# A Hyena layer in a vision tower: three band buffers, moved sums, gated products summed by four column groups and reordered through DRAM

## What is computed

```python
u = jnp.einsum('bld,ed->ble', inputs, w_in) + b_in
...  # short filter of three taps; split by head into x0, x1, v
kv = x1[..., i] * v[..., j]          # outer product of the channels of a head
y[i] = x0[j] * causal_conv(kv[i, j], h)   # summed over the j channels of the head
...  # RMS norm over the 192 channels, then w_out, b_out and the residual
```

## Time and profile before

| | us |
|---|---|
| median of 3 executions | 706.13 |
| lowest, highest | 704.66, 707.17 |
| the profiled execution | 707.24 |
| its span, first to last instruction | 705.5 |
| mean granted clock of PE in it | 0.975 of full speed |
| PE, DVE, ACT, POOL busy | 598.2, 286.9, 199.4, 146.3 |
| the Hyena part, from PE's first turn of rows to the first rows for the router | 498.8 to 593.8 |

### The profile page before, as it was taken

The page is one execution under the profiler, slowest core; times in us unless marked ns, Lnnn a source line. Parts: engine busy times, 40 slices in busy tenths (PEclk is TensorE's granted clock), DMA queues, the critical chain, the costliest instruction groups (busy, mean ns, idle before and its releaser), DMA issues. The chain is left out here.

```text
span 705.5 us, 10938 instructions
## 1 busy us (share of the span) xinstructions
PE 598.2 (85%) x4299; PEld 434.5 (62%) x4305; DVE 286.9 (41%) x662; ACT 199.4 (28%) x479; POOL 146.3 (21%) x215
## 2 busy tenths in 40 slices
PE   1023979999999989878999999999867999979996
PEld 1001749555555543334999999989534557649995
DVE  0000042467768647796043333345395125202221
ACT  2001242144444433242434443310341002112220
POOL 6771110011111102342000000002063212312222
PEclk9999999999999999999999999999997999989998
DMA  7506132000000000410987777100633791346650
GB/s 200 170 5 266 71 102 68 1 1 1 2 1 1 2 0 1 133 47 1 320 315 296 291 293 276 68 1 1 243 130 88 279 342 67 108 158 194 187 174 1
DMA packets 26667, 86.55 MB, mean 123 GB/s; under 512 B 7182, under 2 KB 16551, under 8 KB 21498
## 3 DMA queue, kind: packets, MB, share of 16 engines
q1 hardware_dynamic: 23946, 82.70, 33.8%
q0 software_dynamic: 2672, 3.17, 1.6%
HBM read 79.49 MB, written 7.04 MB: 123 GB/s over the span
## 5 line engine op out<-in xcount | busy, mean ns | idle before, releaser
L1556 DVE TENSOR_TENSOR eo<-banks,soft_factors 32x192 f32<-32x192 f32 x128 | 45.3, 354 | 91.7 <-PE banks L1506 71.0
L1537 ACT ACTIVATE ex<-banks,soft_b 128x128 f32<-128x128 f32 x192 | 51.2, 399 | 73.3 <-PE banks L1492 73.2
L889 DVE TENSOR_REDUCE nm<-banks 128x1 f32<-128x453 f32 x96 | 55.9, 624 | 31.6 <-PE banks L662 31.3
L1506 PE MATMUL banks<-soft_pair_w,ex 128*128 128x192 f32 x384 | 66.4, 330 | 1.4 <-issue 1.4
L680 PE MATMUL banks<-qa,kt 32*99 32x256 f32 (+1 forms) x384 | 65.9, 399 | 0.0
L849 ACT ACTIVATE pt<-banks 128x1024 f32<-128x1024 f32 (+1 forms) x48 | 49.1, 1023 | 57.2 <-PE banks L680 57.2
L662 PE MATMUL banks<-kt,qt 32*128 32x453 f32 x192 | 62.5, 590 | 2.3 <-DVE nm L889 0.9
L1506 PEld LDWEIGHTS banks<-soft_pair_w,ex 128*128 128x128 f32 x384 | 62.0, 190 | 3.3 <-issue 1.6
L1487 PE MATMUL banks<-slots_a,soft_pair_w 128*128 128x128 f32 x384 | 45.9, 276 | 1.2 <-PEq L1256 1.1
L1487 PEld LDWEIGHTS banks<-slots_a,soft_pair_w 128*128 128x128 f32 x384 | 44.9, 192 | 2.4 <-issue 2.0
L680 PEld LDWEIGHTS banks<-qa,kt 32*99 32x99 f32 (+1 forms) x384 | 38.3, 172 | 4.0 <-issue 0.8
(11 more groups left out here) (297 smaller groups left out, 1003.6 us busy)
## 6 DMA issues: line engine op xcount, KB each, us to landing
soft_pair_w<-in_spair SPq DMA_DIRECT2D x32, 1152.0 KB, 7.4
hy_band<-in_hband SPq DMA_DIRECT2D x6, 1540.0 KB, 6.7
route_tile_wi<-in_wi SPq DMA_DIRECT2D x15, 576.0 KB
switch_wo<-in_wo SPq DMA_DIRECT2D x1, 4608.0 KB, 15.6
hy_x_spread<-x_rows SPq DMA_DIRECT2D x24, 128.5 KB, 5.2
sorted_x<-blank_rows SPq DMA_DIRECT2D x15, 193.0 KB
route_tile_x<-sorted_x SPq DMA_DIRECT2D x15, 193.0 KB
vt<-in_vt SPq DMA_DIRECT2D x1, 2496.0 KB
```

The lines of the kernel that those rows point to most:

```text
L889: dve.tensor_reduce(nm[:, n % 2, j, at:at + 1], ps[:, q, 0:NK], AXX, ALU.max, negate=True).then_inc(maxed, 1)
L1506: mm = pe.matmul(ps[:, 6 + q, 0:D], hid[:, p % 2, q, j, :], w[:, at:at + D], start=j == 0, stop=j == HJ - 1)
L1537: ins = act.activation(hid[:, p % 2, q, j, :], hidden(p, q, j), ACT.Gelu, bias=k.b1[:, 2 * p + q, j:j + 1])
L1556: dve.tensor_tensor(eo[SL * r:SL * (r + 1), b, i, :], ps[SL * b:SL * (b + 1), 6 + e % 2, 0:D], b2[SL * r:SL * (r + 1), i, :], ALU.add).the ...
```

## The change

Eight things are changed, all in the Hyena layer:

- POOL's two sums to `h` go from behind outer(1) to behind outer(3); outer(1) now waits for the second third's kvz.
- DVE runs `cls_outer(0)` and `cls_outer(1)` ahead of the next tap step each, and PE's `pick_cls(0)` goes ahead of a product.
- There are three band buffers and three x0 buffers instead of two (the third x0 buffer and both `hy_kv` buffers lie in the switch layer's `route_tile_wi`, which is idle then); SP interleaves band and x0 loads and loads the output weights behind them.
- There are six buffers of gated products instead of three.
- `sum_y` is replaced for groups 0 to 4 by `sum_pairs`: when all four pairs of a group are gated, four matmuls with a 32-column selection matrix write to four column groups, 32 rows each, of one bank. Its rows stand in another order (pair, then image). Group 5 keeps the old form (`sum_last`).
- ACT copies such a bank to `hy_y_by_pair`, stores its four quarters to a DRAM tensor `y_rows` and, once all four are stored, loads them back in the old order into `hy_y`.
- The squares of groups 0 to 4 are first added up by POOL (`add_squares`, behind all outer products; slots of two and a sum), and PE handles them once; the last group's are handled as before. ACT waits for POOL's add before it overwrites a slot.
- PE's `project(0, c)`, and DVE's class rows of y, wait for the load of that group (`y_moved`).

```diff
 for g in range(NG):
     if g % 2 == 0:
         pool.wait_ge(x.xr, 4 * (g // 2 + 1))
+    if g == 1:
+        pool.wait_ge(x.kvz_r, 2)
     if g >= 2:
         pool.wait_ge(conv, GP_ * (g - 1))
     for s in range(JT):
         outer(g, s)
-    if g == 1:
+    if g == 3:
         pool.wait_ge(x.wout_in, 32)
         pool.tensor_tensor(k.h[:, :, :], k.h[:, :, :], bc(x.bout[:, :], 1, NT),
                            ALU.add).then_inc(h0, 1)
         pool.wait_ge(h0, 1)
         pool.tensor_tensor(k.h[:, :, :], k.h[:, :, :], k.xn[:, :, :], ALU.add).then_inc(h1, 1)
+for c in range(1, NG - 1):
+    add_squares(c)
...
+def add_squares(c):
+    pool.wait_ge(ysq_r, c + 1)
+    if c >= 2:
+        pool.wait_ge(ysa_r, c - 1)
+    pool.tensor_tensor(ysq[:, 2, :], ysq[:, 0 if c == 1 else 2, :], ysq[:, c % 2, :], ALU.add
+                       ).then_inc(ysa_r, 1)
...
+def sum_pairs(c):
+    wait_y_bank(c)
+    pe.wait_ge(gated, GP_ * (c + 1))
+    for g in range(GP_):
+        mm = pe.matmul(ps[QUAD * g:QUAD * (g + 1), YB + c % 2, 0:L], x.sel_pair,
+                       prod[:, (GP_ * c + g) % PR, :], start=True, stop=True)
+    mm.then_inc(ysum, GP_)
...
     cls_source(m)
     cls_source(m + 1)
     convolve(m)
-    if m >= 2:
-        sum_y(m - 2)
-        sum_y(m - 1)
     convolve(m + 1)
+    if m % GP_ == 0 and m >= GP_:
+        sum_pairs(m // GP_ - 1)
+    if m == PAIRS - 2:
+        sum_last(PAIRS - 4)
+        sum_last(PAIRS - 3)
...
-    if m >= GP_ and m % GP_ == 2:
-        squares(m // GP_ - 1)
-sum_y(PAIRS - 2)
-sum_y(PAIRS - 1)
+pe.wait_ge(ysa_r, NG - 2)
+squares(2, x.image_pair, x.tail_pair, True)
+sum_last(PAIRS - 2)
+sum_last(PAIRS - 1)
...
 for c in range(NG - 1):
-    pe.wait_ge(y_r, c + 1)
+    pe.wait_ge(y_moved[c % 2], 16 * (c // 2 + 1))
     project(0, c)
...
+def store_y(c):
+    r = c % 2
+    act.wait_ge(yp_r, c + 1)
+    if c >= 2:
+        act.wait_ge(y_moved[r], 16 * (c // 2))
+    for g in range(GP_):
+        act.dma_start(y_rows[r, :, g, :, :], y_pair[QUAD * g:QUAD * (g + 1), r, :]
+                      ).then_inc(y_stored[r], 16)
+def load_y(c):
+    r = c % 2
+    act.wait_ge(y_stored[r], 16 * GP_ * (c // 2 + 1))
+    act.dma_start(y[:, c, :], y_rows[r].rearrange("b g n l -> (b g n) l")).then_inc(y_moved[r], 16)
 for c in range(NG):
     act.wait_ge(ysum, GP_ * (c + 1))
-    act.activation(ysq[:, c, :], ps[:, YB + c % 2, 0:L], ACT.Square).then_inc(ysq_r, 1)
+    if c >= 2:
+        act.wait_ge(ysa_r, max(1, c - 2))
+    act.activation(ysq[:, c % 2, :], ps[:, YB + c % 2, 0:L], ACT.Square).then_inc(ysq_r, 1)
...
+    act.activation(y_pair[:, c % 2, :], ps[:, YB + c % 2, 0:L], ACT.Copy, scale=x.nw_pair[:, c:c + 1]
+                   ).then_inc(yp_r, 1)
+    store_y(c)
+    load_y(c)
```

More of the change, by code:

```diff
@@ L1639, in __init__ @@
         self.x1, self.v = (sb(n, [P, JT, NH * B * CH]) for n in ("x1", "v"))
[L1640 to L1641 removed]
+        self.band = sb("band", [P, BRING, HG, BANDW])
+        spread = sb("x0_spread", [P, 2, GP_, L])
+        self.xrep = [spread[:, 0, :, :], spread[:, 1, :, :],
+                     k.route.wi[2][:, 0:GP_ * L].rearrange("p (u l) -> p u l", u=GP_)]
         consts = sb("consts", [P, MIXC])
@@ L1709, in sync @@
         sp.dma_start(x.consts[:, :], a["hconsts"]).then_inc(x.const_in, 16)
[L1710 to L1713, removed]
+        x.load_band(sp, a, 0)
         sp.wait_ge(x.c2, W_X0 + 1)
@@ L1716, in sync @@
         sp.wait_ge(x.x0_out, 16)
-        for g in range(2):
-            x.load_x0(sp, g)
+        x.load_x0(sp, 0)
+        x.load_band(sp, a, 1)
+        x.load_x0(sp, 1)
+        sp.dma_start(x.wout[:, :, :], a["hwout"]).then_inc(x.wout_in, 16)
+        sp.dma_start(x.bout[:, :], a["hbout"].broadcast_to([P, D])).then_inc(x.wout_in, 16)
+        x.load_band(sp, a, 2)
+        x.load_x0(sp, 2)
         sp.wait_ge(x.c2, W_X0_REST + 1)
@@ L1879, in stage_hyena @@
         rms = sb("hy_rms", [P, NT])
-        zeroed, kv_r, conv, gated = (k.sem(f"hy_{n}") for n in ("zeroed", "kv_ready", "conv", "gated"))
+        zeroed, kv_r, conv, gated, ysa_r, yp_r = (k.sem(f"hy_{n}") for n in (
+            "zeroed", "kv_ready", "conv", "gated", "squares_added", "y_by_pair"))
+        y_stored = [k.sem(f"hy_y_stored{r}") for r in range(2)]
+        y_moved = [k.sem(f"hy_y_moved{r}") for r in range(2)]
+        y_rows = nc.dram_tensor("y_rows", (2, B, GP_, 2 * CH, L), F32, kind="Internal").ap()
         ysum, y_r, ysq_r, yc_r, ms_m, mse_r, rms_r = (
@@ L1890, in _ @@
                 k.route.load(sp, a)
-                for g in range(2, NG):
-                    sp.wait_ge(conv, GP_ * (g - 1))
+                for g in range(BRING, NG):
+                    sp.wait_ge(conv, GP_ * (g - BRING + 1))
                     x.load_band(sp, a, g)
-                    sp.wait_ge(gated, GP_ * (g - 1))
+                    sp.wait_ge(gated, GP_ * (g - BRING + 1))
                     if g == P // (2 * CH * GP_):
@@ L1978, in squares, with sum_last @@
+                def sum_last(m):
+                    if m % GP_ == 0:
+                        wait_y_bank(NG - 1)
+                    pe.wait_ge(gated, m + 1)
+                    pe.matmul(ps[:, YB + (NG - 1) % 2, 0:L], x.sel[:, m % GP_, :], prod[:, m % PR, :],
+                              start=m % GP_ == 0, stop=m % GP_ == GP_ - 1).then_inc(ysum, 1)
+                def squares(slot, image, tail, first):
+                    if first:
                         pe.wait_ge(zeroed, 1)
```

109 lines of the change are left out of this document (63 added, 46 removed).

## The result

The changed kernel takes 703.23 us (median; 700.01 to 706.75) against 707.62 for the kernel before on the same chip (704.49 to 709.87), a ratio of 0.9943, 95% interval 0.9921 to 0.9964. Faster, as forecast, but by 4.4 us instead of the 9.1 that the sum gave, and just above the range of 689 to 703 (the measured median is 703.2; 0.9943 of 706.13 would be 702.1).

The account below looks back on a forecast made before the run. Bound: DVE's chain with POOL's sums before the Hyena loop, then PE alone to 586.6. With ACT's round trip as the new limit, shift -10.6 plus 1.5 clock loss gave -9.1: 698.1, or 697.0 as median; range 689 to 703.

Parts of the forecast that it names:

- A, the start: Before the Hyena loop: PE's first class row at 523.5, 9.6 us earlier, without the gap, convolutions then at 2.4 GHz.
- B, PE's loop: PE's Hyena loop: the sum over four column groups takes 0.64 us, so a group takes 5.98 us instead of 8.22.
- step D: ACT's DRAM round trip: 5.65 us a hop, 4.8 more for group 2's stores beside the weights; last load lands at 575.6.
- C: POOL's add behind its last outer product makes ACT wait: group 2's square starts at 552.0, not at 546.3.
- the rival of held products: POOL's moved sums hold DVE's gated products 3.8 us twice, PE stalls 2 to 3 us: 699.5 us; chance 0.05.
- E: Fifth projection step: load of y at 575.6 against 586.24, shift -10.6; clock loss 1.5, so -9.1 us in sum.
- Quiet stores: ACT's stores slip between the weight rows: no 4.8 us delay, clock loss 0.5, so -14.9, 691.2 us; chance 0.25.
- Long hops: Stores of one group queue behind each other, 5.2 us instead of 2.5 in three hops: -4.8, 701.3 us; chance 0.13.
- Slower than before: Every DRAM hop costs 11.0 us, group 4's load lands at 590.1: +6.4 with the clock, 712.5 us; chance 0.03.

Follow-up runs that it names:

- The repeat: The changed kernel run once more, unedited, on the chip of the experiments; ratio to the kernel before 0.9954.
- start-only kernel: The kernel before with only the moved POOL sums and outer(1), and the earlier DVE and PE class steps; ratio 0.9873.
- the first two with ACT freed: The changed kernel with each group's load behind the next group's stores and separate square slots; ratio 0.9801 with expert weights late, 0.9886 with them early.

## Why the prediction was right and wrong

**A, the start: right.** 523.5 predicted for the first class row, 522.93 measured, full clock, no gap. (The repeat has no gap either, but its clock fell behind the first gated product.) The first gated product cost PE 1.31 us, not 0.6. In the start-only kernel A came to 7.1 us of stage, where that product's wait was 1.94 and half clock followed, so some of the 9.6 was given back there.

**B, PE's loop: right.** 0.64 for the sum over four column groups. PE's rows of the sum stand at 533.65, 539.26 and 544.87, 5.6 apart, a little under 5.98. The gain couldn't be cashed, as step D below says.

**C: right in size, wrong in place.** POOL's rows:

```profile
539.02 3.85 POOL L1952 TENSOR_TENSOR h<-h,hy_b_out 128x1728 f32<-128x1728 f32 x1
542.95 3.85 POOL L1955 TENSOR_TENSOR h<-h,xn 128x1728 f32<-128x1728 f32 x1
546.76 4.29 POOL L1923 TENSOR_TENSOR route_tile_wi<-hy_x,hy_v 128x512 f32<-128x512 f32 x4
551.01 0.63 POOL L1938 TENSOR_TENSOR hy_y_square<-hy_y_square 128x257 f32<-128x257 f32 x1
```

The add ends at 551.6, where I had 551.75. The cover of outer(4) was thin by 0.41 us (PE's wait for it at 549.07) instead of spare by 0.6. But ACT didn't come for the third square until 566.91; it was held by the stores and not by this add. Without the late bands it happened as foretold: third square 17.3 us after the first (547.00 - 529.70), predicted 552.0 - 534.3 = 17.7. Gated products beside the sums kept their 0.42, so the rival of held products is out:

```profile
541.60 0.43 DVE L2152 TENSOR_TENSOR hy_prod<-banks,route_tile_wi 128x257 f32<-128x257 f32 x1 [1.80 <-PE banks L1985]
```

**D failed, in one term: which stores are congested, and by how much.** I gave groups 0 and 1 quiet stores and charged group 2 with 4.8. I had asked only what the weight load would do, dated it right (546.5, measured 545.47), and then put the wrong store beside it and cut the hold off at 562.1, its landing when it took 15.6 us as before. Three terms were wrong:

- The bands, which I had put at nothing. A quicker PE brings 1.5 MB every 5.6 us, and group 0's stores met them: 9.15 us instead of 2.16.
- Group 1's stores, at 548, were the ones beside the weights, and were held to their end: 16.28 us.
- That end is 566.3, for the weights are slowed too, and land in 20.8 us instead of 15.6.

The high bound should have been: a store issued behind the weights may be through only when they are, and nothing in the trace of before spoke against that. With group 1 held to 566.46, group 2 began at 566.91 instead of 552.0, 14.9 later, and the 4.8 charged to it fell away. From its square to the last load's issue it was 15.4 us (566.91 to 582.31) and not 16.4, and that load took 2.0 and not 2.4: 14.9 - 4.8 - 1.0 - 0.4 = 8.7. It was through at 584.3, and predicted for 575.6. Of the excess of 21.1, the add at 552.0 would have covered 6.4 in any case (552.0 - 534.3 - 2 x 5.65).

**E: right in size, wrong in what PE waits for.** PE was to wait some 4 us before the squares and, longest, before the fifth projection step, for the load of y. Before the squares it did wait, 3.04 us; for the load of y it never did. The end of the chain in the trace of the change, from POOL's last add on:

```profile
577.94 0.65 POOL hy_y_square L1938
578.63 0.39 PE banks L2017 x2
...
582.18 3.51 PE banks L2057 x40
```

PE waits for POOL's last add, and then works at half clock (0.50 from 580 to 584): the five projection steps take 3.51 us, where they took 1.84, and it comes to the fifth at about 582.18 + 4/5 of 3.51 = 585.0, when the load has been there for 0.7 us. Both the add and the load hang on the same square of group 4 (577.47), so the late stores are to blame either way. At full clock the load would have set the end, 584.3 + 1/5 of 1.84 = 584.7; PE ended at 585.7. So the clock cost 1.0, for which I took 1.5. The end of the steps is 0.9 earlier than before (586.61), and so are the router's rows (592.27 and 593.13), where the sum had 9.1.

**What lies behind the stage** I had left as it was, and it gave 3.6 us in the first pair of traces and 1.6 in the second (112.4 to 110.8). Of the 3.6, 1.3 is the landing of the last scatter (POOL's idle time before the first tile 6.16, then 4.89, with the scatters issued alike) and most of the rest PE's clock: in the windows from 626 to 632, before and after,

```profile
626.00:632.00 6.00, 4.91 (x26) 4.24 (x28) 0.00 (x0) 1.40 (x6) 0.19 (x1) 0.50 0.37 111
```

```profile
626.00:632.00 6.00, 5.22 (x53) 4.70 (x52) 1.11 (x2) 1.77 (x7) 0.00 (x0) 1.00 0.35 120
```

PE did 26 matmuls at half speed, or 53 at full. Why the unedited part fares better is open. The kernel before with late weights had 111.1 there, so it isn't bound to the change. Of the difference between the spans, then, the stage has a quarter in the first pair of traces (1.1 of 4.5) and half in the second (2.2 of 4.3). That the measured time came so near the range is luck: 9.1 was forecast for the stage, and 1.1 and 2.2 (88.66 to 86.43) came.

**The rivals.** Quiet stores would have been 14.9 us faster, and with weights late and no late bands the stage was 16.3 shorter: the mechanism was computed about rightly, its condition wasn't met. "Long hops" came nearest in time, 701.3, by another mechanism: hops weren't all long, two were very long. The chance on it was too small because I had taken the congestion as a matter of one hop. "Slower than before" has a slip in its sum: with hops of 11.0 group 2 starts at 534.3 + 2 x 11.0 = 556.3 and no longer at 552.0, so its time should stand 4.3 later; from hops of 8.9 on (17.7 / 2) they set that start and not the add. And the two stores that landed at 2.3 to 2.7 when alone are of 128.5 KB each, not 64.

## What to carry to other kernels

When a change speeds up the engine that sets the pace, list every transfer that it triggers and write down when each is issued and when it lands under the new pace; a small round trip that must pass among them is priced by what is queued before it (here up to 14 us above its own 2.2), not by its own size. Where a chain through DRAM is needed, put the bulk load behind it with one wait: here that line gave 10 us of stage. And test the parts alone: the start of this change alone was better than the whole (0.9873 against 0.9943).

## What was unexpected of the hardware

- Four stores of 32 KB from ACT's queue are through 2.2 us after the last issue in quiet, and after 5.3 to 16.3 us with bands, x0 and weights from SP's queue going on. Stores whose issue began 2.8 us (first execution of the change) and 8.0 us (second) behind the 4.6 MB load were through 0.2 and 1.7 us after it. But the single store of 128.5 KB that was issued 0.93 us behind that load was through 11.4 us before it. In the kernel with ACT freed and early weights a load of y, issued 0.25 us behind it at 514.37, passed it as well: it took 6.9 us, and the weights were there only at 536.2. What decides between the two is open.
- The Trainium skill (DMA: Bandwidth & Descriptors, "Issuing engines are not separate DMA queues") has transfers of all issuing engines interleave on the same 16 DMA engines. That transfers of ACT and SP slow each other down the runs show, with the numbers above and below. Small transfers that pass a large load they show only where these were issued within 1 us of it; of those issued 2.8 us or more behind it, undivided, none whose landing the chains of waits show was through before it was.
- It costs the load as well: 4.6 MB in 15.6 us in the kernel before, without such stores, and 20.8 us in the change, with stores, a band and x0 beside it; the DMA share was 1.07 at 406 GB/s from 535 to 555.
- The narrow store isn't the issue, though it is narrow: ACT's queue has 1440 packets in the profile after, 1280 rows of stores and loads and 160 more.
- An issue on ACT takes 0.60 us for the quarter stores (four in 2.49), 0.33 for the load; beside the bands the first four took 3.34.
- The same 1.31 us wait of PE for the first gated product was followed by full clock in one execution of the changed kernel (1.00 from 531 to 540) and by a fall of the clock in the other (0.62 over the same stretch). The wait is the same 1.31 in six experiments on the changed kernel: with late weights the clock fell (0.58 from 501 to 509), with short rows, with the single store, without late bands and in the first two with ACT freed it did not (1.00 in the 8 us behind the wait). Why is open.
